# Threshold search of a fused attention and feed-forward block: folded weights, a bit in PSUM, later loads of the natural weights

## What is computed

```python
def _perturb_attractive(w, scale=SCALE, sparsity=SPARSITY):
    a = jnp.abs(w)
    s = jnp.sort(a.ravel())
    n = s.shape[0]
    k = max(1, int(n * sparsity / 2))
    thr_bot = s[k - 1]
    thr_top = s[n - k]
    tier = jnp.where(a >= thr_top, -1.0, jnp.where(a <= thr_bot, 1.0, 0.0))
    return w + scale * w * tier
```

## Time and profile before

| | us |
|---|---|
| median of 3 runs | 242.56 (241.97 to 242.58) |
| the profiled execution | 242.93 |
| its span in the profile | 241.2 |
| busy: TensorE, VectorE, ScalarE, GpSimd | 213.4, 191.7, 169.2, 143.5 |
| mean granted clock of TensorE, share of full speed | 0.986 |

### The profile page before, as it was taken

The page is one execution under the profiler, slowest core; times in us unless marked ns, Lnnn a source line. Parts: engine busy times, 40 slices in busy tenths (PEclk is TensorE's granted clock), DMA queues, the critical chain, the costliest instruction groups (busy, mean ns, idle before and its releaser), DMA issues.

```text
span 241.2 us, 5510 instructions
## 1 busy us (share of the span) xinstructions
PE 213.4 (88%) x1856; PEld 145.1 (60%) x1856; DVE 191.7 (79%) x584; ACT 169.2 (70%) x402; POOL 143.5 (59%) x231
## 2 busy tenths in 40 slices
PE   7985998989988978978969988996989999999993
PEld 2653656655655655655657655564554879766793
DVE  2688799999889999999897888778596577658364
ACT  2477758999998998998966967984666940453320
POOL 8632060576978987997584433653869916283800
PEclk9999799999999999999997999999999999999999
DMA  6558644994735525523432500000000000010011
GB/s 175 129 153 240 145 114 129 224 264 130 190 89 132 137 71 136 147 75 99 117 90 65 139 0 7 0 3 3 0 3 0 3 0 25 24 43 0 3 43 43
DMA packets 19299, 20.44 MB, mean 85 GB/s; under 512 B 1384, under 2 KB 17527, under 8 KB 18207
## 3 DMA queue, kind: packets, MB, share of 16 engines
q1 hardware_dynamic: 18582, 19.76, 31.1%
q10 hardware_dynamic: 688, 0.33, 0.5%
HBM read 14.70 MB, written 5.26 MB: 83 GB/s over the span
## 4 chain that ended last, share of the span: by engine, by line
PE 46%; DVE 29%; ACT 13%; issue 8%; DMA 2%; SPq 0%; ACTq 0%; DVEq 0%
PE bank L914 12%; PE bank L896 8%; DVE nmax L1199 7%; ACT msk L597 6%; DVE msk L1170 4%; PE bank L819 3%; ACT PT L585 3%; PE bank L715 3%; DVE cand L1182 3%; PE bank L945 2%; DVE nmax L1195 2%; PE bank L776 2%; PE bank L879 2%; DMA ob<-in_wmod 2%; PE bank L798 2%
## 5 line engine op out<-in xcount | busy, mean ns | idle before, releaser
L495 POOL TENSOR_SCALAR_AFFINE_SELECT PT<-PT 128x256 f32<-128x256 f32 (+1 forms) x96 | 45.9, 495 | 37.2 <-ACT PT L585 35.4
L585 ACT ACTIVATE PT<-bank 128x512 f32<-128x512 f32 x96 | 54.9, 606 | 4.3 <-PE bank L793 3.4
L1199 DVE TENSOR_REDUCE nmax<-bank 128x2 f32<-128x512 f32 x64 | 43.3, 682 | 2.1 <-PE bank L776 1.5
L597 ACT ACTIVATE msk<-w2a,cand 128x512 bf16<-128x512 f32 x60 | 42.9, 725 | 0.0
L461 POOL TENSOR_TENSOR ex<-eul,lg 128x32 f32<-128x32 f32 x4 | 21.8, 5438 | 16.6 <-DVE lg L1261 16.6
L597 ACT ACTIVATE msk<-w1a,cand 128x512 bf16<-128x512 f32 x31 | 22.7, 733 | 6.0 <-DVE cand L1182 5.8
L1195 DVE TENSOR_REDUCE nmax<-bank 128x4 f32<-128x512 f32 x32 | 21.6, 676 | 5.0 <-PE bank L769 4.8
L798 PE MATMUL bank<-Qs,Ks 80*128 80x256 bf16 x128 | 24.8, 276 | 0.6 <-ACT PT L585 0.2
L776 PE MATMUL bank<-Ks,Qs 78*128 78x256 bf16 x128 | 24.8, 276 | 0.0
L1170 DVE TENSOR_SCALAR_CACHE_REDUCE msk<-w1a,cand 128x512 bf16<-128x512 f32 x31 | 23.1, 745 | 1.2 <-DVE cand L1182 0.2
L772 PE MATMUL bank<-mask 128*128 128x256 bf16 x64 | 17.9, 279 | 6.3 <-DVE nmax L1199 5.2
(11 more groups left out here) (197 smaller groups left out, 510.5 us busy)
## 6 DMA issues: line engine op xcount, KB each, us to landing
Qs<-parts SPq DMA_DIRECT2D x7, 576.0 KB
Ks<-parts SPq DMA_DIRECT2D x7, 576.0 KB
parts<-part SPq DMA_DIRECT2D x7, 384.0 KB, 3.0
rows_bc<-rows_out SPq DMA_DIRECT2D x8, 192.0 KB, 7.6
x_all<-in_x SPq DMA_DIRECT2D x8, 128.0 KB, 6.1
parts<-part SPq DMA_DIRECT2D x8, 128.0 KB, 3.1
out<-ob SPq DMA_DIRECT2D x3, 256.0 KB, 2.3
w_sb<-in_w SPq DMA_DIRECT2D x2, 256.0 KB, 5.0
```

Source lines behind the costliest of these rows:

```text
L495: gp.affine_select(out=v, in_=v, compare_op=ALU.is_ge, fill=0.0, base=0, pattern=[[0, v.shape[1]], [1, P]], channel_multiplier=-1).then_in ...
L585: act.activation(PT[:, e % 2, j], psE[u % 2][:, :], ACT.Exp).then_inc(q["exp_done"], 1)
L597: act.activation(msk[:, col], w[:, :], ACT.Sign, bias=cand[:, col:col + 1].bitcast(F32), scale=-(1.0 - 2.0 ** -24), accum_out=acc[:, col:c ...
L1199: ve.tensor_reduce(nmax[:, b % 2, 1, h:h + 2], bank.rearrange("p (h k) -> p h k", h=2), axis=AX.X, op=ALU.max, negate=True).then_inc(q["ma ...
```

## The change

Both weights lie folded in one tile `wa` of 128 x 1024: W1 on partitions 0 to 63, W2 on 64 to 127. A candidate column then serves one threshold of both weights, each half of the partitions its own, and there are two columns: TOP and BOT. ScalarE takes a sign over all 1024 columns for TOP and over the first 512 for BOT; VectorE counts the other 512 for BOT into a tile of its own, `acc_d`, whose TOP column holds a constant so that both columns are compared with one number. TensorE adds over halves of the partitions with two products into the same place: first VectorE's counts by a matrix with twos, then, behind the wait for ScalarE, ScalarE's by one with ones.

`decide` writes the bit, already at its place, into PSUM beside the totals; `next_cand` merges it with the candidate itself. `after_next`, `nxt`, `probe`, `ktab` and their loads and constants go. The bank is given on when the candidate is written, not when the bit is decided. The matrices for the sums are filled by twelve instructions at the head of VectorE's stream; the first candidate by one on GpSimd.

The natural weights are loaded later, behind the second `other_rows` of SyncE's list. The thresholds go through DRAM (two writes, one read) to reach all partitions, between the last two `max_rows`. `find_tiers` first takes the absolute value of the natural weight, into `w1p` and `w2p`. `gate_signs` moves from before the loop to the end of step 0, and `other_mod_rows` waits for it.

```diff
-VEC_STEP, ROWS_STEP, SIZE_STEP, BIAS_STEP, WO_STEP = 0, 1, 7, 31, 7
+SIGNS_STEP, VEC_STEP, ROWS_STEP, SIZE_STEP, BIAS_STEP, WO_STEP = 0, 0, 1, 7, 31, 7
...
-POOL_SETS = 18
-
-
-def alone(n):
-
-    return SLOT[n] >= 0
+POOL_SETS = 9
+HALF_SETS = 12
+HALF = P // 2
+ON_ACT = FF
+TOP, BOT = 0, 1
+SIGNED_TOP = 2 * (P * FF - K_STAT) - P * FF
+SIGNED_BOT = 2 * (K_STAT - 1) - HALF * ON_ACT
...
-        ones_f = sb("ones_f", [P, P])
+        halves = sb("halves", [P, 2, P])
...
-        w1a = sb("w1a", [P, FF])
-        w2a = sb("w2a", [P, FF])
+        wa = sb("wa", [P, 2 * FF])
...
-        acc = sb("acc", [P, 4])
-        ktab = sb("ktab", [P, 2, 4])
-        cond = sb("cond", [P, 4], U32)
-        cur = sb("cur", [P, 4], U32)
-        cand = sb("cand", [P, 4], U32)
-        nxt = sb("nxt", [P, 4], U32)
-        probe = sb("probe", [P, NBITS + 1, 4], U32)
+        acc = sb("acc", [P, 2])
+        acc_d = sb("acc_d", [P, 2])
+        cand = sb("cand", [P, 2], U32)
+        cur = sb("cur", [P, 2], U32)
+        thr = sb("thr", [P, 4], U32)
...
+        bits_x = psX[:, B1_COLS - 8:B1_COLS - 6].bitcast(U32)
...
-            sp.dma_start(w1_sb[:, :], w1).then_inc(q["w1_in"], 16)
-            sp.dma_start(w2_sb[:, :, :], w2.rearrange("(c p) d -> p c d", p=P)).then_inc(q["w2_in"], 16)
+            sp.dma_start(wa[0:HALF, :], w1.rearrange("(p r) f -> p (r f)", r=2)).then_inc(q["wa_in"], 16)
+            sp.dma_start(wa[HALF:P, :], w2.rearrange("(p r) d -> p (r d)", r=8)).then_inc(q["wa_in"], 16)
             sp.dma_start(wmod_sb[:, 2 * D:6 * D], wmod[:, 2 * D:6 * D]).then_inc(q["modrow_in"], 16)
-            sp.dma_start(probe.rearrange("p n c -> p (n c)"), probe_c.partition_broadcast(P)).then_inc(q["probe_in"], 16)
...
+            def thresholds():
+
+                sp.wait_ge(q["cand_done"], NBITS + 1)
+                sp.dma_start(thr_dram[0:1, :], cur[0:1, :]).then_inc(q["thr_out"], 16)
+                sp.dma_start(thr_dram[1:2, :], cur[HALF:HALF + 1, :]).then_inc(q["thr_out"], 16)
+                sp.wait_ge(q["thr_out"], 32)
+                sp.dma_start(thr[:, :], thr_dram.rearrange("a b -> (a b)").partition_broadcast(P)).then_inc(q["thr_in"], 16)
...
             other_rows(1)
+            sp.dma_start(w1_sb[:, :], w1).then_inc(q["w1_in"], 16)
+            sp.dma_start(w2_sb[:, :, :], w2.rearrange("(c p) d -> p c d", p=P)).then_inc(q["w2_in"], 16)
...
             max_rows(B - 2)
+            thresholds()
             max_rows(B - 1)
...
-            gp.memset(ones_f[:, :], 1.0).then_inc(q["pool_set"], 1)
+            gp.memset(cand[:, :].bitcast(F32), 2.0 - 2.0 ** -23).then_inc(q["cand_done"], 1)
...
-            low, high = K_STAT - 1, P * FF - K_STAT
-            signed = lambda k: 2 * k - P * FF
-            for r, ks in enumerate(((low, high, signed(high), signed(low)), (low, signed(high), signed(high), signed(low)))):
-                for col, k in enumerate(ks):
-                    gp.memset(ktab[:, r, col:col + 1], float(k)).then_inc(q["pool_set"], 1)
...
-            def sign_count(n, col, w):
+            def sign_count(n, col, width):
+                if n == 0:
+                    act.wait_ge(q["wa_dve"], 1)
                 act.wait_ge(q["cand_done"], n + 1)
                 if n:
                     act.wait_ge(q["tot_done"], n)
-                act.activation(msk[:, col], w[:, :], ACT.Sign, bias=cand[:, col:col + 1].bitcast(F32),
+                scratch = msk[:, 2 * col:2 * col + width // FF].rearrange("p a f -> p (a f)")
+                act.activation(scratch, wa[:, 0:width], ACT.Sign, bias=cand[:, col:col + 1].bitcast(F32),
                                scale=-(1.0 - 2.0 ** -24), accum_out=acc[:, col:col + 1]).then_inc(q["m_act"], 1)
...
+                act.wait_ge(q["dve_set"], SETS["sgn"])
...
-            act.wait_ge(q["w1_in"], 16)
-            act.activation(w1a[:, :], w1_sb[:, :], ACT.Abs).then_inc(q["act_set"], 1)
+            act.wait_ge(q["wa_in"], 32)
+            act.activation(wa[:, 0:FF], wa[:, 0:FF], ACT.Abs).then_inc(q["wa_act"], 1)
             first_parts()
-            sign_count(0, 2, w1a)
+            act.wait_ge(q["wa_act"], 1)
+            sign_count(0, TOP, 2 * FF)
...
-            act.wait_ge(q["w2a_done"], 1)
-            sign_count(0, 3, w2a)
+            sign_count(0, BOT, ON_ACT)
             scaled(1)
-            sign_count(1, 2, w1a)
+            sign_count(1, TOP, 2 * FF)
             high_parts(1)
-            sign_count(1, 3, w2a)
+            sign_count(1, BOT, ON_ACT)
...
-                    sign_count(n, 2, w1a)
-                if n is not None:
-                    sign_count(n, 3, w2a)
-                    if alone(n):
-                        sign_count(n, 1, w2a)
+                    sign_count(n, TOP, 2 * FF)
+                    sign_count(n, BOT, ON_ACT)
...
-                pe.wait_ge(q["m_act"], signs_through(n))
-                claim_x((q["cond_done"], n + 1))
-                mm(psX[:, 0:4], ones_f[:, :], acc[:, :], start=True, stop=True).then_inc(q["tot_done"], 1)
+                if n == 0:
+                    pe.wait_ge(q["half_set"], HALF_SETS)
+                claim_x((q["cand_done"], n + 2))
+                mm(psX[:, 0:2], halves[:, 1, :], acc_d[:, :], start=True, stop=False)
+                pe.wait_ge(q["m_act"], 2 * (n + 1))
+                mm(psX[:, 0:2], halves[:, 0, :], acc[:, :], start=False, stop=True).then_inc(q["tot_done"], 1)
...
+            def half_sums():
+
+                for i in range(2):
+                    for lo, hi in ((0, HALF), (HALF, P)):
+                        for left, right in ((0, HALF), (HALF, P)):
+                            ve.memset(halves[lo:hi, i, left:right], float(i + 1) if lo == left else 0.0).then_inc(q["half_set"], 1)
+                for lo in (0, HALF):
+
+                    ve.memset(acc_d[lo:lo + 32, TOP:TOP + 1], (SIGNED_BOT - SIGNED_TOP) / 64).then_inc(q["half_set"], 1)
+                    ve.memset(acc_d[lo + 32:lo + HALF, TOP:TOP + 1], 0.0).then_inc(q["half_set"], 1)
+
+            half_sums()
...
-            def first_cand():
-                v.wait_ge(q["probe_in"], 16)
-                ve.tensor_copy(cand[:, :], probe[:, 0, :]).then_inc(q["cand_done"], 1)
-                ve.tensor_copy(nxt[:, :], probe[:, 1, :]).then_inc(q["nxt_done"], 1)
-
             def dve_counts(n):
                 v.wait_ge(q["cand_done"], n + 1)
-                for col, w in ((0, w1a),) if alone(n) else ((0, w1a), (1, w2a)):
-                    last = ve.tensor_scalar(msk[:, col], w[:, :], cand[:, col:col + 1].bitcast(F32), 0.0, op0=ALU.is_lt,
-                                            op1=ALU.add, accum_out=acc[:, col:col + 1])
-                last.then_inc(q["m_dve"], 1)
+                ve.tensor_scalar(msk[:, 3], wa[:, ON_ACT:2 * FF], cand[:, BOT:BOT + 1].bitcast(F32), 0.0, op0=ALU.is_le,
+                                 op1=ALU.add, accum_out=acc_d[:, BOT:BOT + 1]).then_inc(q["m_dve"], 1)
 
             def decide(n):
                 v.wait_ge(q["tot_done"], n + 1)
-                ve.tensor_tensor(cond[:, :], psX[:, 0:4], ktab[:, int(alone(n)), :], op=ALU.is_le).then_inc(q["cond_done"], 1)
+                ve.tensor_scalar(bits_x, psX[:, 0:2], float(SIGNED_BOT), float(1 << (NBITS - 1 - n)), op0=ALU.is_le,
+                                 op1=ALU.mult).then_inc(q["cond_done"], 1)
 
             def next_cand(n):
-                bit = NBITS - 1 - n
+                flip = (1 << (NBITS - 1 - n)) >> 1
                 v.wait_ge(q["cond_done"], n + 1)
-                v.wait_ge(q["nxt_done"], n + 1)
-                ve.scalar_tensor_tensor((cand if bit else cur)[:, :], cond[:, :], bit, nxt[:, :], op0=ALU.logical_shift_left,
+                ve.scalar_tensor_tensor((cand if flip else cur)[:, :], cand[:, :], flip, bits_x, op0=ALU.bitwise_xor,
                                         op1=ALU.bitwise_or).then_inc(q["cand_done"], 1)
-
-            def after_next(n):
-                ve.tensor_tensor(nxt[:, :], cand[:, :], probe[:, n + 2, :], op=ALU.bitwise_xor).then_inc(q["nxt_done"], 1)
...
-            def find_tiers(a, top, bot):
+            def find_tiers(ready, w, a, top, bot):
 
                 t0, t1 = msk[:, 0], msk[:, 1]
+                v.wait_ge(q[ready], 16)
+                then_self(absolute(a, w))
                 v.wait_ge(q["cand_done"], NBITS + 1)
+                v.wait_ge(q["thr_in"], 16)
                 then_self(ve.tensor_scalar(t0, a, top.bitcast(F32), None, op0=ALU.is_ge))
...
-            first_cand()
-            v.wait_ge(q["w2_in"], 16)
-            absolute(w2a[:, :], w2_sb.rearrange("p c d -> p (c d)")).then_inc(q["w2a_done"], 1)
+            v.wait_ge(q["wa_in"], 32)
+            absolute(wa[:, FF:2 * FF], wa[:, FF:2 * FF]).then_inc(q["wa_dve"], 1)
             first_split()
-            v.wait_ge(q["w2a_done"], 1)
-            v.wait_ge(q["act_set"], ACT_SETS["w1a"])
+            v.wait_ge(q["wa_dve"], 1)
...
+                if t == SIGNS_STEP:
```

(21 more changed lines are left out.)

15 lines of the change are left out of this document (6 added, 9 removed).

## The result

Beside each other on one chip the kernel before took 242.45 us (median, 241.97 to 242.58) and the kernel after 240.39 us (239.84 to 249.56); the ratio is 0.9906, 95% interval 0.9881 to 0.9931. Two later series gave 0.9826 (0.9785 to 0.9866) and 0.9854 (0.9784 to 0.9924). The mean of the three, 0.986, is 3.3 us of 242.5; forecast were 4.2 us, 238.4, in a range of 233.5 to 242.5. Times are medians over all executions, but ratios leave out those more than 1.5% above the fastest of their kernel, which show a lower granted clock: 5 of 16 of the kernel after, whose mean over all 16 is 242.4 us, and 4 of 67 of the kernel before, with 242.5; what brings them on stays open, so that the gain is one of the other executions alone.

What follows compares the result with a forecast made beforehand. VectorE was taken to pace the middle of the search, ScalarE and TensorE later. Start -1.15 and -0.4, 27 to 43 us +0.3, 43 to 111 us -3.3, 111 to 162 us -0.1, tiers +0.45: -4.2, 238.4 us, range 233.5 to 242.5.

Steps and rivals of the forecast that it cites:

- The start, -1.15: First search bits: a 0.85 us hold of L1182 goes and ScalarE's signs are 0.30 shorter, together 1.15 us gained.
- The start's clock, -0.4, and +0.3 up to bit 7: TensorE's shorter pause may keep its clock, 0.4 gained; in 27 to 43 us three later totals outweigh removed work, +0.3.
- The holds in 43 to 111 us, -2.3: Middle of the search: all GpSimd holds of L1182 vanish with one operand in PSUM, 2.3 us gained over 15 bits.
- L1186, -3.1: Search, 43 to 111 us: this small VectorE instruction goes; of its 4.24 us, 3.1 us are gained.
- The product, 7 x 0.3 = +2.1: Search, 43 to 111 us: TensorE's second float32 product costs 0.3 us on 7 of the 15 bits.
- ScalarE's signs: Search: one long and one short sign replace three, saving 0.30 us a bit; counted as -1.6 in 111 to 162 us.
- 111 to 162 us, -0.1: Last 9 search bits: shorter ScalarE signs gain 1.6 us, five later totals on the chain cost 1.5.
- The tiers, +0.45: Step 33, behind the search: remaking W1's absolute value on VectorE costs 0.45 us; a GpSimd hold could add up to 1.
- Rival 1: More is won: the second product lies wholly in TensorE's pauses and the start's clock holds, -9.9, 232.7 us; chance 0.17.
- Rival 2: The holds of L1182 stay, or the last instruction is held in its turn: 241.9 us; chance 0.10.
- Rival 4: Slower: the total paces every bit, a loss from 0.285 us per bit, 245.9 us at 0.4; chance 0.11.
- Rival 3: TensorE's product, 0.59 us on half of 29 bits, costs 8.6 against gains of 8.7: 242.4 us; chance 0.12.

Runs made afterwards that it cites:

- the run on the kernel before: The kernel before with only its four comparison bits written to PSUM instead of SBUF: 240.66 us against 241.70, ratio 0.9969.
- the one on the kernel after: The kernel after with only the search bit moved back from PSUM to SBUF: 243.54 us against 242.84 for the kernel before, ratio 1.0002.

## Why the prediction was right or wrong

The sign, the range and the mechanism of the search were right; the size, 4.2 us, was 3.3 in the mean of three series and 2.3 in the first. That it came so near is in part luck. In the first pair of profiles 3.1 us of span went, and 1.27 of them lie ahead of bit 0 and up to 0.9 in a fall of the clock in the kernel before, both not the change's; in this pair they make up for most of what was missed, a term for the tiers that was 2.5 us too low and a gain in the middle that was 1.0 us too high. By its steps:

- *The start, -1.15.* Measured -1.09 (0 to 2), and the holds' -1.04 of it by themselves. Right.
- *The start's clock, -0.4, and +0.3 up to bit 7.* Measured -0.13 together. In this execution TensorE's clock still fell, to 0.50 from 20 to 22 us and 0.69 in the next two, so nothing came from it; in one of three profiles of the kernel after it held, as the prediction's half chance has it, but that is worth 0.4 to 0.9 us, not 1.6.
- *The holds in 43 to 111 us, -2.3.* The holds are gone, all of them, as forecast. Their worth was 1.05 us by the run on the kernel before and 1.74 by the one on the kernel after. The prediction counted busy time as path time.
- *L1186, -3.1.* The worst term of the search: 1.45 us for the same stretch, by putting one like it back. It is the step "so 4.24 - 15 x 0.075 = 3.1 us" that failed: it took the whole of a hold as on the chain, though the chain's own share of L1186 in the earlier trace rows is 3.8% of 68.0, 2.6 us.
- *The product, 7 x 0.3 = +2.1.* Measured 2.26. Right in sum, and in kind: some bits pay and some don't, only ten at about 0.2 rather than seven at 0.3.
- *ScalarE's signs.* I gave them nothing in that stretch. The terms measured above sum to -1.74 - 1.45 + 2.26 = -0.9 against -2.26 for the whole; the missing 1.3 us may be the signs' (0.30 us a bit, ScalarE 4.0 us less busy), or the terms, each measured alone, don't add up. No run took the signs alone, so that stays open.
- *111 to 162 us, -0.1.* Measured -1.28, of which up to 0.9 is the clock in that one execution of before; so -0.4 or more.
- *The tiers, +0.45.* The step that failed in kind: "W1 costs 0.45". It costs 0.4 us as work where L1239 isn't held and 0.7 to 1.0 where it is; such a hold the prediction had named. What it had not is the granted clock, which falls behind TensorE's pause in some executions, 1.0 to 2.2 us more. The prediction asked what is late next on VectorE, not how long TensorE would stand.
- *Loads and thresholds at nothing.* Nothing waits for them in the trace; loading early again was not tried.

Of the signs that the prediction named, the step between bits 7 and 22 is 4.40 us long instead of 4.55, where it said 4.3 and 4.5. Rival 1 is excluded by the product's price, 3.1 us between bits 0 and 30. Rival 2 is excluded by 156 ns in L1194. Rival 4 did not come: 0.15 us a bit in the mean between bits 7 and 22, not the 0.285 from which it would be a loss. Rival 3's mechanism was at work at a good third of its price of 8.6 us; the prediction's 242.4 for it leaves out the tiers' 0.45, with which its sum comes to 242.9. Of the two rules named in the prediction, the Trainium skill (SBUF — State Buffer, Who interferes with whom) was borne out by both runs: one SBUF input, no hold, 156 and 162 ns. The other, the Trainium skill (VectorE: DVE Perf Modes, The TRN2 errata), with its 62 cycles more for a PSUM source, was not: the same instruction took 156 ns with a PSUM operand and 161 with the bit in SBUF (the last one, never held).

## What to carry to other kernels

If a small VectorE instruction is long now and then, look for GpSimd beside it, and give it one operand in PSUM. Count on about half of a removed hold or small instruction where several engines are over 85% busy (here 0.4 to 0.6 of it), until a run says more. When work moves onto a late engine, look at the pause that it makes on TensorE and at the granted clock behind it in more than one execution, and try it in a step in which that engine idles.
